# Searched network of a gated Flamingo stack: first statistics, beta and the last pairs' finish in other places

## What is computed

```python
x = x + tanh(g_xattn[1]) * L1_xattn(layernorm(x), ctx, ctx, mask)     # the second attention
x = x + tanh(g_ffn[1])   * L1_ffn(layernorm(x), ...)                  # the searched network

# L1_ffn: six nodes, each of three earlier nodes
q = ew[c,0] * (nodes[in_q] @ We[eq] + be[eq])    # k and v likewise
o = mha(q, k, v, Wq[c], Wk[c], Wv[c], Wo[c])     # 8 heads of 32
nodes[c] = act_w[c] * o + q
...
return (out - mean) * rsqrt(var + 1e-6) * ln_g + ln_b     # of the last node
```

## Time and profile before

| | |
|---|---|
| median of 3 runs | 3306.04 us (3302.68 to 3307.13) |
| the profiled execution's own time | 3280.64 us |
| its span, first to last instruction | 3278.6 us |
| second attention (first added batch to last residual) | about 714 to 887 us |
| searched network (first statistics to last beta) | 891.5 to 2065.7 us |
| mean granted TensorE clock | 0.954 |

### The profile page before, as it was taken

The page is one execution under the profiler, slowest core; times in us unless marked ns, Lnnn a source line. Parts: engine busy times, 40 slices in busy tenths (PEclk is TensorE's granted clock), DMA queues, the critical chain, the costliest instruction groups (busy, mean ns, idle before and its releaser), DMA issues. The chain is left out here.

```text
span 3278.6 us, 61233 instructions
## 1 busy us (share of the span) xinstructions
PE 3059.5 (93%) x23568; PEld 2333.0 (71%) x23568; DVE 2007.5 (61%) x4366; ACT 1460.9 (45%) x2828; POOL 631.8 (19%) x911
## 2 busy tenths in 40 slices
PE   8987799989899999999999998599999999788999
PEld 6865466567689999999999998367667666456443
DVE  3446111127677877778788776366666666687564
ACT  3431111115545555555555554266666676354000
POOL 3535200025100120013013001311111110144000
PEclk9987899989899999999999999699999999798899
DMA  8642133237500000000000000100000000075000
GB/s 239 192 161 67 56 113 116 97 117 239 195 1 1 2 1 1 2 2 2 1 1 2 1 2 1 50 20 16 21 20 20 20 21 6 4 233 166 12 17 17
DMA packets 76096, 184.95 MB, mean 56 GB/s; under 512 B 12213, under 2 KB 18738, under 8 KB 75476
## 3 DMA queue, kind: packets, MB, share of 16 engines
q1 hardware_dynamic: 57316, 137.48, 13.2%
q10 hardware_dynamic: 12160, 28.80, 2.8%
q0 software_dynamic: 6336, 14.76, 1.6%
HBM read 153.40 MB, written 27.79 MB: 55 GB/s over the span
## 5 line engine op out<-in xcount | busy, mean ns | idle before, releaser
L2333 DVE CUSTOM_DVE_ANT_0 probs<-ps,add 112x375 f32<-112x375 f32 x512 | 250.0, 545 | 58.7 <-PE ps L2461 54.9
L2389 ACT ACTIVATE probs<-probs,neg_top 112x375 f32<-112x375 f32 x512 | 281.8, 599 | 4.7 <-DVE neg_top L2333 3.4
L1884 DVE TENSOR_REDUCE top<-ps 112x16 f32<-112x1792 f32 x96 | 194.3, 2024 | 60.0 <-PE ps L2100 58.6
L1318 DVE TENSOR_TENSOR hidden<-gated,ps 128x512 f32<-128x512 f32 x64 | 44.0, 688 | 303.2 <-PE ps L1361 303.2
L2996 PE MATMUL ps<-we,xn_t 128*112 128x512 f32 x512 | 227.3, 606 | 0.4 <-DVE x_sb L2914 0.4
L2486 PE MATMUL ps<-ident,probs 112*125 112x112 f32 x1536 | 222.5, 281 | 2.8 <-DVE probs_t L2340 2.8
L2340 DVE COPY probs_t<-ps 125x336 f32<-125x336 f32 x256 | 128.6, 502 | 151.6 <-PE ps L2486 151.6
L2486 PEld LDWEIGHTS ps<-ident,probs 112*125 112x125 f32 x1536 | 189.7, 188 | 30.7 <-issue 22.6
L1900 DVE TENSOR_TENSOR probs<-probs,inv_sum 112x1792 f32<-112x1792 f32 x96 | 194.4, 2025 | 3.3
L1888 DVE TENSOR_TENSOR probs<-ps,top 112x1792 f32<-112x1792 f32 x96 | 194.3, 2024 | 3.3
L1896 DVE TENSOR_REDUCE row_sum<-probs 112x16 f32<-112x1792 f32 x96 | 193.9, 2020 | 3.2 <-ACT probs L1986 3.2
(11 more groups left out here) (408 smaller groups left out, 6346.6 us busy)
## 6 DMA issues: line engine op xcount, KB each, us to landing
ctx_t<-in_ctx_T_dram SPq DMA_DIRECT2D x128, 375.0 KB, 3.7
ctx_sb<-in_ctx_dram ACTq DMA_DIRECT2D x72, 384.0 KB, 4.2
ctx_sb<-in_ctx_dram SPq DMA_DIRECT2D x32, 384.0 KB, 4.7
queue<-zeros SPq DMA_DIRECT2D x32, 256.0 KB, 4.3
rows<-queue SPq DMA_DIRECT2D x16, 512.0 KB, 5.0
outputs<-out SPq DMA_DIRECT2D x16, 512.0 KB, 2.9
mask_in<-in_mask_BxSxS_fk_dram SPq DMA_DIRECT2D x16, 328.1 KB, 5.8
mask_in<-in_mask_BxSxS_ik_dram SPq DMA_DIRECT2D x16, 328.1 KB, 6.1
```

The costliest lines, as they stand in the source:

```text
L1884: dve.tensor_reduce(top[:, :, :], scores, AX.X, ALU.max).then_inc(s["top_done"], 1)
L2333: dve.tensor_tensor_reduce(out=probs[:, u, h, :], in0=k.ps[0:S, SCORE + h, 0:L], in1=add[:, j % 2, :], scale=1.0, scalar=BIG, op0=ALU.add, ...
L2389: act.activation(probs[:, u, h, :], probs[:, u, h, :], ACT.Exp, bias=neg_top[:, u, h:h + 1], scale=-1.0).then_inc(s["probs_done"], 1)
```

## The change

1. The eight first batches' statistics are taken in the second attention: VectorE runs `next_statistics(j - 11)` at the end of iterations 11 to 18, and GpSimd takes epsilon and power after its last own work there. The buffers `net.mean_var` and `net.rstd` are new; the temporary ones are those of the mixture (`w.stats`, `w.var_eps`), and to make room `token_scales` no longer has `both_eps` but uses `var_eps` twice, with two more waits on GpSimd.
2. Beta is added to `x` four slots before the last node of the pair, by GpSimd, as soon as the pair's own input has been transposed. It is no longer the last of `add_final`.
3. `add_final` is parted in `scale_final` (epsilon, power) and the rest. For pairs 12 to 15 GpSimd does `scale_final` alone, and VectorE does the rest in `finish_tail`: two `scalar_tensor_tensor` a batch.

```diff
 # token_scales
-        pool.tensor_scalar(w.both_eps[:, cut], w.mean_var[:, cut, 1], 1.0 + RMS_EPS, LN_EPS * RMS_EPS, ALU.mult, ALU.add)...
+        pool.tensor_scalar(w.var_eps[:, cut], w.mean_var[:, cut, 1], 1.0 + RMS_EPS, LN_EPS * RMS_EPS, ALU.mult, ALU.add)...
...
+        pool.wait_ge(s["xr_scales_done"], g + 1)
+        pool.wait_ge(s["scale_step"], 4 * g + 2)
         pool.tensor_scalar(w.var_eps[:, cut], w.mean_var[:, cut, 1], LN_EPS, None, ALU.add).then_inc(s["scale_step"], 1)
 # gathered_attention, gpsimd, at its end
+                pool.wait_ge(net.s["mean_done"], NB)
+                pool.tensor_scalar(w.var_eps[:, 0:NB], net.mean_var[:, :, 1], LN_EPS, None, ALU.add).then_inc(net.s["eps_added"], 1)
+                pool.wait_ge(net.s["eps_added"], 1)
+                pool.tensor_tensor(net.rstd[:, :], w.var_eps[:, 0:NB], k.neg_half[0:S, 0:NB], ALU.pow).then_inc(net.s["rstd_done"], 1)
+                pool.wait_ge(net.s["rstd_done"], 1)
 # gathered_attention, vector
+                def next_statistics(j):
+                    dve.wait_ge(s["residual_done"], j + 1)
+                    dve.bn_stats(w.stats[:, j, :], batch(k.x_sb, j)).then_inc(net.s["stats_done"], 1)
+                    dve.wait_ge(net.s["stats_done"], j + 1)
+                    dve.bn_aggr(net.mean_var[:, j, :], w.stats[:, j, :]).then_inc(net.s["mean_done"], 1)
...
+                    if 0 <= j - LAG - NB < NB:
+                        next_statistics(j - LAG - NB)
 # searched_network
+        beta_at = {last_item(g) - STREAMS: g for g in range(GROUPS)}
+        TAIL = GROUPS - STREAMS
 # gpsimd
+                def add_beta(g):
+                    pool.wait_ge(s["input_transposed"], g + 1)
                     for b in range(PAIR):
                         x = batch(k.x_sb, PAIR * g + b)
-                        pool.wait_ge(s["fin_added"], PAIR * g + b + 1)
                         pool.tensor_tensor(x, x, w.beta[:, :], ALU.add).then_inc(s["beta_added"], 1)
-                pool.wait_ge(s["mean_done"], NB)
-                pool.tensor_scalar(var_eps[:, :], mean_var[:, :, 1], LN_EPS, None, ALU.add).then_inc(s["eps_added"], 1)
-                pool.wait_ge(s["eps_added"], 1)
-                pool.tensor_tensor(rstd[:, :], var_eps[:, :], k.neg_half[0:S, 0:NB], ALU.pow).then_inc(s["rstd_done"], 1)
                 for t in range(SLOTS):
                     if t in stats_at:
                         normalise_input(stats_at[t])
                     if t in final_at:
+                        scale_final(final_at[t])
+                    if t in final_at and final_at[t] < TAIL:
                         add_final(final_at[t])
+                    if t in beta_at:
+                        add_beta(beta_at[t])
 # vector
-                for j in range(NB):
-                    dve.bn_stats(stats[:, j, :], batch(k.x_sb, j)).then_inc(s["stats_done"], 1)
-                for j in range(NB):
-                    dve.wait_ge(s["stats_done"], j + 1)
-                    dve.bn_aggr(mean_var[:, j, :], stats[:, j, :]).then_inc(s["mean_done"], 1)
...
+                def finish_tail(g):
+                    u = g % 2
+                    dve.wait_ge(s["fin_rstd_done"], g + 1)
+                    for b in range(PAIR):
+                        dve.scalar_tensor_tensor(fin[:, u, b, :], fin[:, u, b, :], fin_mean_var[:, u, b, 0:1], w.gamma[:, :],
+                                                 ALU.subtract, ALU.mult).then_inc(s["fin_tailed"], 1)
+                    dve.wait_ge(s["beta_added"], PAIR * (g + 1))
+                    for b in range(PAIR):
+                        x = batch(k.x_sb, PAIR * g + b)
+                        dve.wait_ge(s["fin_tailed"], 2 * PAIR * (g - TAIL) + b + 1)
+                        dve.scalar_tensor_tensor(x, fin[:, u, b, :], fin_rstd[:, u, b:b + 1], x, ALU.mult, ALU.add).then_inc(s["fin_tailed"], 1)
...
                     if t in final_at:
                         final_statistics(final_at[t])
+                        if final_at[t] > TAIL:
+                            finish_tail(final_at[t] - 1)
...
+                finish_tail(GROUPS - 1)
+                dve.wait_ge(s["fin_tailed"], 2 * PAIR * STREAMS)
 # scalar, copy_final
-                    if g >= 2:
+                    if 2 <= g < TAIL + 2:
                         act.wait_ge(s["fin_added"], PAIR * (g - 1))
+                    if g >= TAIL + 2:
+                        act.wait_ge(s["fin_tailed"], 2 * PAIR * (g - 1 - TAIL))
```

More of the change, by code:

```diff
@@ L867, in searched_storage @@
     net.be_s = sb(nc, "be_s", [P, NODES, 3, DC], F32)
-    names = "scalars_loaded rows_loaded be_scaled rows_scaled ends_scaled"
+    net.mean_var = sb(nc, "net_mean_var", [S, NB, 2], F32)
+    net.rstd = sb(nc, "net_rstd", [S, NB], F32)
+    names = "stats_done mean_done eps_added rstd_done scalars_loaded rows_loaded be_scaled rows_scaled ends_scaled"
     net.s = {n: sem(nc, n) for n in names.split()}
@@ L929, in token_scales @@
         pool.wait_ge(s["mean_done"], (g + 1) * G)
-        pool.tensor_scalar(w.both_eps[:, cut], w.mean_var[:, cut, 1], 1.0 + RMS_EPS, LN_EPS * RMS_EPS, ALU.mult, ALU.add).then_inc(s["scale_step"], 1)
+        pool.tensor_scalar(w.var_eps[:, cut], w.mean_var[:, cut, 1], 1.0 + RMS_EPS, LN_EPS * RMS_EPS, ALU.mult, ALU.add).then_inc(s["scale_step"], 1)
         pool.wait_ge(s["scale_step"], 4 * g + 1)
-        pool.tensor_tensor(w.xr_scale[:, cut], w.both_eps[:, cut], neg_half, ALU.pow).then_inc(s["xr_scales_done"], 1)
+        pool.tensor_tensor(w.xr_scale[:, cut], w.var_eps[:, cut], neg_half, ALU.pow).then_inc(s["xr_scales_done"], 1)
     elif part == 1:
-        pool.tensor_tensor(w.r_inv[:, cut], w.both_eps[:, cut], half, ALU.pow).then_inc(s["scale_step"], 1)
+        pool.tensor_tensor(w.r_inv[:, cut], w.var_eps[:, cut], half, ALU.pow).then_inc(s["scale_step"], 1)
+        pool.wait_ge(s["xr_scales_done"], g + 1)
+        pool.wait_ge(s["scale_step"], 4 * g + 2)
         pool.tensor_scalar(w.var_eps[:, cut], w.mean_var[:, cut, 1], LN_EPS, None, ALU.add).then_inc(s["scale_step"], 1)
@@ L1826, in normalise_input, with scale_final @@
                                            ALU.subtract, ALU.mult).then_inc(s["in_normed"], 1)
-                def add_final(g):
+                def scale_final(g):
                     u = g % 2
@@ L1857, in _ @@
                     if t in final_at:
+                        scale_final(final_at[t])
+                    if t in final_at and final_at[t] < TAIL:
                         add_final(final_at[t])
+                    if t in beta_at:
+                        add_beta(beta_at[t])
             @block.vector
             def _(dve):
+                dve.wait_ge(w.s["mean_done"], NB)
+                dve.wait_ge(w.s["rstd_done"], 1)
                 for j in range(NB):
-                    dve.bn_stats(stats[:, j, :], batch(k.x_sb, j)).then_inc(s["stats_done"], 1)
-                for j in range(NB):
-                    dve.wait_ge(s["stats_done"], j + 1)
-                    dve.bn_aggr(mean_var[:, j, :], stats[:, j, :]).then_inc(s["mean_done"], 1)
-                dve.wait_ge(s["mean_done"], NB)
-                dve.wait_ge(s["rstd_done"], 1)
-                for j in range(NB):
-                    dve.tensor_scalar(first_input(j // PAIR)[:, j % PAIR, :], batch(k.x_sb, j), mean_var[:, j, 0:1], rstd[:, j:j + 1],
+                    dve.tensor_scalar(first_input(j // PAIR)[:, j % PAIR, :], batch(k.x_sb, j), w.mean_var[:, j, 0:1], w.rstd[:, j:j + 1],
                                       ALU.subtract, ALU.mult).then_inc(s["normed"], 1)
@@ L1916, in final_statistics @@
                     if g >= 2:
+                        dve.wait_ge(s["fin_rstd_done"], g - 1)
+                    if 2 <= g < TAIL + 2:
                         dve.wait_ge(s["fin_normed"], PAIR * (g - 1))
+                    if g >= TAIL + 2:
+                        dve.wait_ge(s["fin_tailed"], 2 * PAIR * (g - 1 - TAIL))
                     for b in range(PAIR):
```

12 lines of the change are left out of this document (5 added, 7 removed).

## The result

Five runs of the changed kernel have a median of 3286.0 us (3283.95 to 3294.43); five of the kernel before 3307.13 (3302.68 to 3308.48). The ratio is 0.994, 95% interval 0.9926 to 0.9954: 21.1 us saved, 15 to 24 by the interval, where 15.1 were forecast. The time lies in the range and on the side forecast, but the saving is 6 us larger, and that needs an explanation as much as a miss would.

What follows compares the result with a forecast made beforehand. TensorE was taken to bound most of the searched network, so only its two ends could give time: -5.46 + 2.3 - 12.0 = -15.1 us, from 3306.04 to 3290.9 us, range 3284 to 3299.

Steps and rivals of the forecast that it cites:

- Start: Network's start: everything between 891.48 and 896.94 leaves, as the first statistics are taken earlier; -5.46 us.
- The rival that the start gives nothing: Network's start: TensorE's program arrives late or another wait fills the idle, only the end counts; 3296.3 us, chance 0.10.
- a granted clock that comes out better after the shorter idle: Network's start: allowance of 2 us in the range's lower edge, the price of one iteration at the lower clock level.
- Moved statistics: Second attention: pairs in iterations 11 to 14 cost nothing, four in 15 to 18 cost 0.58 us each; +2.3 us.
- Token scales: Two more waits in each of four groups on GpSimd: nothing, at most four times about 0.1 us.
- Beta in the middle: Middle of the network: beta's adds on GpSimd change place and not length, 1.41 us fit an idle of 2.28; nothing.
- End: Network's end, pairs 12 to 15: VectorE's finishing ends at 2053.65 against GpSimd's 2065.69; -12.0 us.
- sign of 8 us: Network's end, in the changed profile: next load comes 8 us after TensorE's last matmul, not 21.
- the end doesn't hold the next block: Rival: another engine or queue leaves the network late, so the end's 12.0 us are void; 3302.9 us, chance 0.08.
- The slower clock: Rival, second attention from iteration 15: TensorE's clock falls to the lower level and stays; up to 3327 us, chance 0.05.
- The ports' case: Rival, network's end: GpSimd's last three powers with epsilon, about 1 us each, exclude finishing instructions; 3294 us, chance 0.08.
- The carry-over: Median 25.4 us above the profiled execution, unexplained from one trace; the saving of 15.1 us is carried over unchanged.

Runs made afterwards that it cites:

- before once more: The kernel before, no edit, run again for a second profiled execution: 3311.36 us, ratio 1.0008 to the other runs of this kernel on this chip.

## Why the prediction was right

**Start, -5.46 forecast: right.** The step to the first transpose went from 11.2 to 5.9 us, -5.3, and in the other pairs of profiles from 11.4 to 5.9. The rival that the start gives nothing is out: nothing took the place of the statistics. What I had allowed for below, a granted clock that comes out better after the shorter idle, did not come: the clock still starts at 0.50 in the first 4 us of the changed network.

**Moved statistics, +2.3 forecast: the size right, the condition missing.** The first uncovered pair costs 0.53 us for 0.58; iterations 15 to 19 take 2.4 us more, and the move to earlier iterations gives them back. What fails is "the delay is carried to the end" as a statement for every execution. It was read from one in which VectorE never stood between iterations 15 and 23. On the first chip it stands 2.17, 2.17 and 0.77 us before iteration 17 in the three profiles without the moved pairs, and nothing in the two profiles with them and the long routing, and the term is 0.3 to 1.7 us. I had looked for slack on TensorE's rows, and they show none: they end 3.1 us before what waits for them goes on.

**Token scales, 0: right**, within 0.9982 to 1.0012 of no change; GpSimd's order there is off the path.

**Beta in the middle, 0: right in time**, to 0.2 us of 1043, **but not as argued.** I had said that beta changes place and not length. Six of GpSimd's 32 adds fall beside VectorE's product of line 1915 (1900 in the kernel before) and take 1.93 to 1.94 us for 0.73, and once VectorE's product waits for GpSimd. The two lines by their sources (minimum, median and maximum in ns), and the timeline where VectorE stands:

```profile
L1868 POOL TENSOR_TENSOR x_sb<-x_sb,beta x32: 722/727/1941, 919.2 to 1829.7; 112x256 f32<-112x256 f32 x32
L1915 DVE TENSOR_TENSOR probs<-probs,inv_sum x96: 2024/2025/4833, 936.6 to 2049.2; 112x1792 f32<-112x1792 f32 x96
```

```profile
1824.88 5.51 POOL L1868 TENSOR_TENSOR x_sb<-x_sb,beta 112x256 f32<-112x256 f32 x8
...
1827.44 4.83 DVE L1915 TENSOR_TENSOR probs<-probs,inv_sum 112x1792 f32<-112x1792 f32 x1
```

GpSimd runs eight adds without a gap to 1830.39, and VectorE's product ends 1.88 us after them, 2.8 us late. It is so in all six profiles with beta in the middle (4.83 to 4.86 us), and in none of the others (2.03 us at most). TensorE is the bound there, with no idle above 0.14 us around it, so nothing of it reaches the time. **Beta at the start** I had not costed at all. Its first pair waits only for TensorE's transpose of that pair, which is done while VectorE still normalises; there it costs TensorE 0.26 us.

**End, -12.0 forecast: -12.9 measured** between the first two profiles (1085.14 to 1072.25), -11.8 against before once more. The mechanism is as forecast, pair by pair. The term mis-sized is `finish_tail`, taken as 4 x 0.484 = 1.94 us, of which I had said that overlap might take 0.3. The instructions last 453 to 480 ns, as assumed, but follow each other faster than that: from the first of `finish_tail(14)`, at 2070.41, to the first of `finish_tail(15)`, at 2071.97, are 1.56 us for four. Three of these groups, of 13, 14 and 15, lie on the path: 3 x 0.38 = 1.1 us less. The prediction's sign of 8 us from TensorE's last matmul to the load does not follow from its own sum, which gives 2053.65 + 1.44 - 2045.81 = 9.3; that 8.3 were measured is these 1.1 us. From VectorE's end at 2073.64 to the load are 1.63 us, where GpSimd's end left 1.44.

**The rivals.** That the end doesn't hold the next block is out: the load follows VectorE's last instruction. The slower clock did not come: 1.00 with TensorE busy 17.06 of 20 us. The ports' case is true, but not where I had priced it. At the end GpSimd's epsilon and power stretch from 0.23 and 0.73 to 0.36 and 0.80 us beside VectorE's new instructions, which keep their 0.48; 0.2 us a pair and not the microsecond of the rival, and not on the path: the last pair's power ends at 2071.83, and VectorE needs it at 2072.76. At the start VectorE is the one that is slowed, from 0.41 to 0.82 us, and GpSimd keeps its 0.73. I could have read that before: I had argued from line 1900, which never varies in the kernel before, beside a GpSimd instruction of another kind: in nine of its 96 cases GpSimd normalises, a `tensor_scalar`, and neither engine is longer for it, while the add of beta, a `tensor_tensor`, stretches one or the other. And the instruction of the same kind as `xn` at line 301, in the first attention of before (its source view, the same columns as above), does:

```profile
L301 DVE TENSOR_SCALAR xn<-x_sb,mean_var,rstd x32: 397/406/727, 23.1 to 177.8; 112x256 f32<-112x256 f32 x32
```

The Trainium skill, page "SBUF — State Buffer", section "SBUF: two separate sides", has the port pair as an exclusive lock, held for a whole instruction. Between the adds of beta and line 1915 the trace agrees: each of the six long adds ends 0.58 or 0.59 us after VectorE's product, and the long product ends 1.88 us after GpSimd's last add, as if each had waited for the other's end and then run. Elsewhere it doesn't: a factor of 2 on both `xn` while the adds beside them keep their length, a stretch of 0.1 us on GpSimd at the end, and nothing between the normalising and line 1900 are not what whole instructions waiting for each other would give in these rows.

**The sum.** By stages it is -5.3 + 2.4 + 0.3 - 12.9 = -15.5 us with the short kind of routing, and with 0.3 for 2.4, the least that the profiles of the first chip allow, -17.6. The two timed results are -21.1 (-24 to -15) and -14.1 (-19 to -9), and both sums lie in both intervals. What stays open is whether the first result holds some 4 us more than the parts show; no profile has a stage for them, and the parts run apart (statistics with token scales -2.0, the rest -14.9, by their ratios) sum to -16.9. Open as well is what makes routing long or short: all four profiles of one chip had the long kind and all four of the other the short kind, what waits for TensorE's matmuls goes on up to 9.9 us after their end in the long kind and 0.04 us after it in the short one, and no run here varied anything in it.

**The carry-over** from 3280.64 to 3306.04 was right to do and I could not say why. Most of it is the routing phase, 182.4 us in the profile of before and 198.0 to 204.5 in the profiles of the first chip, and with it VectorE's wait before iteration 17: both outside the change, so that a difference carries over and a level doesn't.

## What to carry to other kernels

A delay that is added to an engine with no idle costs its full length in the execution in which it was read; read a second execution too, here it was 2.4 us in one and 0.3 in another. Work placed at a boundary should be cut where another engine still covers it; the same statistics five iterations earlier cost nothing instead of 2.4 us. The releaser's name in a profile is inferred: look in the kernel for what the instruction waits for, and at the rows of that engine. Where two engines read SBUF side by side, look at the longest of an instruction's durations and not only at its mean. And cut two profiles into stages before comparing their spans: here the faster kernel's was the longer by 7.5 us.

## What was not expected of the hardware

- Beside GpSimd's addition of beta (two SBUF inputs, 112 x 256), VectorE's `tensor_scalar` of the same size takes 809 to 822 ns, alone 405 to 416; GpSimd's takes 0.73 us either way. Beside VectorE's `tensor_tensor` of 112 x 1792 the same addition takes 1.93 us, and behind eight of them that product takes 4.83 us for 2.02. GpSimd's small epsilon and power beside VectorE's `scalar_tensor_tensor` are the other way round: GpSimd is stretched, VectorE not.
- Back to back, four `scalar_tensor_tensor` instructions of 0.45 to 0.48 us take 1.56 us.
- TensorE's matmuls can end, by their rows, up to 9.9 us before an instruction that waits for them goes on (277.32 and 287.20 in the second profile of before), in every profile of one chip and in none of the other.
- One phase of the same kernel, the routing, takes 176 to 182 or 198 to 205 us. The two chips differ by 1% in the time of the kernel before (3308.51 and 3276.15), and 20 to 28 of these 32 us are the length of that phase.
- After an idle of TensorE of 5.5 or 11 us the granted clock starts at 0.50 alike, and comes back at moments that differ by more than a microsecond between executions.
